# A windowed-attention and FFN kernel: a token tile's work is cut into five parts that are issued between the score steps

## The reference

```
x  = layernorm(x)
disp = x @ W_disp   (16 heads x 16);   val = x @ W_val   (16 heads x 64)
strain[t, j] = disp[t - 63 + j] - disp[t]                       # j = 0..63
bond   = gelu(strain @ W_strain + rel[j] @ W_pos) @ W_bond
damage = sigmoid(gelu(strain @ W_dmg + b_dmg) @ W_dmg_out + b_dmg_out)
w = softmax_j(bond - 10 * damage);   att = (sum_j w * val[t - 63 + j]) @ W_cproj
x = x + att
y = layernorm(x); yp = y shifted by one token
out = x + sigmoid((mu_r*y + (1-mu_r)*yp) @ W_r) * (square(relu((mu_k*y + (1-mu_k)*yp) @ W_k)) @ W_v)
```

## Time and profile before

| | |
|---|---|
| median of 3 runs | 3383.02 us (3380.91 to 3383.12) |
| the profiled execution | 3383.59 us, of which the slowest core's span is 3381.7 us |
| spans of the eight cores | 3370.0 to 3381.7 us |
| busy on the slowest core | PE 1703.1, DVE 915.1, ACT 909.3 us |
| tiles 1 to 5 | about 163 to 329 us of the span |
| chunks 0 to 2 with tiles 6 to 17 | about 330 to 1425 us |

### The profile page before, as it was taken

One profiled execution on the slowest core, in us unless ns is written; L12 is line 12 of the kernel. 1 busy time (PEld: TensorE's weight loads), 2 busy tenths in 40 slices (PEclk: granted clock), 3 DMA queues, 4 the chain that ended last, 5 costly groups with the idle time before them and its releaser, 6 DMA issues.

```text
span 3381.7 us, 21888 instructions; the slowest of 8 cores (3370.0 to 3381.7 us)
## 1 busy us (share of the span) xinstructions
PE 1703.1 (50%) x4568; PEld 468.0 (14%) x4568; DVE 915.1 (27%) x2635; ACT 909.3 (27%) x1269; POOL 8.3 (0%) x15
## 2 busy tenths in 40 slices
PE   0054454545554545265555555566634736547367
PEld 0011111111111111011111221222210101101011
DVE  0012333343335333433333222211121030120301
ACT  0001555355554555044440223200011011110110
POOL 0000000000000000000000000000000000000000
PEclk9999656555555565556555555555555555555555
DMA  7500000010001000120001111111210110100101
GB/s 117 104 23 24 10 10 10 4 19 10 10 10 22 10 10 10 19 50 25 25 25 44 35 35 32 37 43 49 56 38 6 38 38 13 55 7 25 44 6 44
DMA packets 133861, 100.42 MB, mean 30 GB/s; under 512 B 110304, under 2 KB 111472, under 8 KB 133744
## 3 DMA queue, kind: packets, MB, share of 16 engines
q1 hardware_dynamic: 126784, 87.80, 9.8%
q0 software_dynamic: 6960, 11.24, 2.4%
HBM read 74.86 MB, written 35.40 MB: 33 GB/s over the span
## 4 chain that ended last, share of the span: by engine, by line
PE 41%; ACT 21%; issue 20%; DVE 12%; DMA 5%; DVEq 1%; ACTq 0%; SPq 0%
ACT s_actT L377 10%; ACT s_actT L367 5%; PE ps L610 5%; PE ps L264 5%; PE ps L708 5%; PE ps L754 5%; PE ps L733 5%; DMA Ebuf<-s_zero 4%; PE ps L386 3%; PE ps L282 2%; DVE s_eh L444 2%; PE ps L542 2%; PE ps L546 2%; PE ps L568 2%; PE ps L562 2%
## 5 line engine op out<-in xcount | busy, mean ns | idle before, releaser
L386 PE MATMUL ps<-s_actT,s_bd 128*32 128x512 bf16 (+1 forms) x1280 | 445.0, 494 | 393.8 <-ACT s_actT L377 325.7
L377 ACT ACTIVATE s_actT<-s_argT,s_pcols 128x512 bf16<-128x512 bf16 (+1 forms) x640 | 368.3, 646 | 13.5 <-ACT s_actT L377 0.4
L377 ACT ACT_TABLE_LOAD x20 | 25.7, 1283 | 914.6 <-DVE s_argT L356 914.6
L367 ACT ACTIVATE s_actT<-s_argT,s_bdmgc 128x2048 bf16<-128x2048 bf16 x128 | 256.3, 2002 | 16.2 <-PE ps L386 7.3
L356 DVE TENSOR_TENSOR s_argT<-s_dS 128x512 bf16<-128x512 bf16 (+1 forms) x640 | 203.5, 379 | 150.5 <-ACT s_actT L377 124.3
L356 DVE TENSOR_TENSOR s_argT<-s_dD 128x512 bf16<-128x512 bf16 (+1 forms) x640 | 203.5, 379 | 146.7 <-ACT s_actT L377 101.1
L708 PE MATMUL ps<-s_xk,s_wkT 128*128 128x512 bf16 x256 | 149.6, 584 | 158.7 <-DVE s_xk L698 76.9
L386 PEld LDWEIGHTS ps<-s_actT,s_bd 128*32 128x32 bf16 x1280 | 123.2, 117 | 712.6 <-issue 693.5
L250 PE MATMUL ps<-s_ident,s_lntok 128*128 128x128 bf16 x136 | 35.9, 264 | 341.2 <-DVE s_lntok L193 323.5
L264 PE MATMUL ps<-s_wval,s_lnfm 128*128 128x512 bf16 x272 | 158.8, 584 | 58.9 <-DVE s_lnfm L254 20.8
L610 PE MATMUL ps<-s_wcp,s_atok 128*128 128x512 bf16 x272 | 158.9, 584 | 57.2 <-DVE s_atok L588 19.1
(11 more groups left out here) (99 smaller groups left out, 1213.9 us busy)
## 6 DMA issues: line engine op xcount, KB each, us to landing
s_wbt<-Ebuf SPq DMA_DIRECT2D x17, 764.0 KB, 5.4
Ebuf<-s_zero SPq DMA_DIRECT2D x16, 544.0 KB
X2buf<-s_xrel SPq DMA_DIRECT2D x17, 512.0 KB, 2.6
s_x<-X2buf SPq DMA_DIRECT2D x17, 512.0 KB, 3.8
s_xt<-xs SPq DMA_DIRECT2D x33, 256.0 KB, 3.9
s_xrel<-xs SPq DMA_DIRECT2D x33, 256.0 KB, 4.2
s_x2r<-X2buf SPq DMA_DIRECT2D x16, 512.0 KB, 3.7
out<-s_x2r SPq DMA_DIRECT2D x16, 512.0 KB, 2.7
```

Of the source, the lines that this page charges most:

```text
L367: P.emit("scalar", (lambda half=half: (lambda e: e.activation(out=s_actT[:, 2048 * half:2048 * half + 2048], in_=s_argT[:, 2048 * half:204 ...
L377: P.emit("scalar", (lambda slot=slot, W=W, bias=bias: (lambda e: e.activation(out=s_act[slot][:, 0:W], in_=s_arg[slot][:, 0:W], func=AF.Ge ...
L386: (lambda e: e.matmul(PS[bank][32 * q:32 * q + 32, 0:W], s_bd32[:, pi * 128 + v * 32: pi * 128 + v * 32 + 32], s_act[slot][:, 0:W], start= ...
```

## The change

`emit_tile` is cut into five functions: `part_ln` (load and LayerNorm), `part_te` (transposes and their copy), `part_val`, `part_disp` and `part_dsd` (the four small matmuls). Their instructions are the same. One wait differs: the transposes of tile b wait for the `val` copies of tile b-1 and no longer for its last copies.

Before chunk 0 only tiles 1 to 4 are issued, sorted by tile number plus 0, 1, 1.5, 2 or 2.5 for the five parts, so that parts of neighbouring tiles alternate. The parts of tiles 5 to 17 go into a queue, 65 in all. In chunks 0 to 2 one part is taken from it after every four steps and one after each combination, that is five for a group. A group thus gets the LayerNorm behind its first bond steps, the transposes behind its first damage steps, `val` behind its second bond steps, `disp` behind its second damage steps and before the combination, and the small matmuls behind the combination. That is 60 parts, tiles 5 to 16; tile 17 follows whole behind chunk 2's dump.

```
-    def emit_tile(b):
+    sv_dscr = {}
+    def part_ln(b):
...
+    def part_te(b):
+        lnt = s_lntok[b % 2]
         bank = b % 2
-        wtp = {"sv": max(ln_done[b], lnfm_evac.get(b - 2, 0), dSD_evac.get(b - 1, 0)),
+        wtp = {"sv": max(ln_done[b], lnfm_evac.get(b - 2, 0), val_evac.get(b - 1, 0)),
...
+    def part_val(b):
...
+    def part_disp(b):
...
-        sv_dscr = P.now("sv")
+        sv_dscr[b] = P.now("sv")
+    def part_dsd(b):
         for m in range(2):
...
-                waits={"sv": max(sv_dscr, P.now("sv"))}, inc="st")
+                waits={"sv": max(sv_dscr[b], P.now("sv"))}, inc="st")
...
+    TPARTS = (part_ln, part_te, part_val, part_disp, part_dsd)
+    TKEYS = (0.0, 1.0, 1.5, 2.0, 2.5)
...
+    pop_hook = [lambda: None]
...
                             Gc[0] = G
+                        pop_hook[0]()
                 st_pair = P.now("st")
...
                 comb_sv, comb_ss = P.now("sv"), P.now("ss")
+                pop_hook[0]()
...
-    for b in range(1, 6):
-        emit_tile(b)
-    emit_chunk(0, [lambda b=b: emit_tile(b) for b in (6, 7, 8, 9)])
-    emit_chunk(1, [lambda b=b: emit_tile(b) for b in (10, 11, 12, 13)])
-    emit_chunk(2, [lambda b=b: emit_tile(b) for b in (14, 15, 16, 17)])
+    for _, b, i in sorted((b + TKEYS[i], b, i) for b in range(1, 5) for i in range(5)):
+        TPARTS[i](b)
+    PQ = [(b, i) for b in range(5, NTB) for i in range(5)]
+    PQc = [0]
+    def pop_part():
+        if PQc[0] < len(PQ):
+            b, i = PQ[PQc[0]]
+            PQc[0] += 1
+            TPARTS[i](b)
+    pop_hook[0] = pop_part
+    emit_chunk(0)
+    emit_chunk(1)
+    emit_chunk(2)
+    while PQc[0] < len(PQ):
+        pop_part()
+    pop_hook[0] = lambda: None
```

More of the change, by code:

```diff
@@ L305, in emit_tile @@
         dSD_evac[b] = P.now("sv")
+    TPARTS = (part_ln, part_te, part_val, part_disp, part_dsd)
+    TKEYS = (0.0, 1.0, 1.5, 2.0, 2.5)
+    def emit_tile(b):
+        for pf in TPARTS:
+            pf(b)
     ctxB = contextlib.ExitStack()
```

## The result

The change makes the kernel slower: 3479.38 us median against 3381.91 us, a ratio of 1.029 (95% interval 1.0278 to 1.0301). The forecast was 3480 us, within 3440 to 3515. The profiled execution took 3480.25 us, and its slowest core has a span 97.0 us longer than before. These are its rows of the page: the span, the two Gelu lines and the table load at the boundaries (the changed kernel's L393, L383 and L402 are L377, L367 and L386 of before).

The account below looks back on a forecast made before the run. ScalarE was taken to bound the groups inside, the tile's serial chain their boundaries. Groups +94, start -42.8, tile 17 +47.3, less about 2 us, on 3383.6 gave 3480 us, range 3440 to 3515.

Parts of the forecast that it names:

- a part hides nothing: In each group: parts are reached only after the Gelu ends, so ScalarE idles; stalls sum to 45.8 against 37.4 us.
- the `val` gap: Behind a group's second four bond steps: ScalarE stalls 16.3 us, of which val itself is 12.4 us.
- The Tanh's gap: Ahead of the combination: the Tanh waits for disp's last matmul, adding 7.2 us to the earlier 1.43 us.
- The ledger: Whole kernel: groups, start and tile 17 together +98.5 us, less about 2 us for fast PE matmuls.
- the groups: Chunks 0 to 2: four groups at +8.4 us and eight at +7.5 us make +94 us.
- the start: Ahead of chunk 0: first Gelu at 288.7 us instead of 331.53, -42.8 us, mostly from tile 5 moving into chunk 0.
- tile 17: Behind chunk 2's dump with nothing beside it: 8.8 us dump DMAs, 4.7 us load, 33.8 us tile, +47.3 us.
- The clock: PE in the groups: last damage step's matmuls fast at 1.02 us, tile matmuls slow except about 2 us saved.
- The faster clock for `val`: Rival: val matmuls behind steps run at PE's fast level, 66 us less, down to 3414 us; chance 0.08.
- Four table loads in a group: ScalarE: Sqrt and Gelu around the LayerNorm, Exp and Gelu around the combination; 1.28 us each, no extra drain.
- The Square behind a Gelu: LayerNorm on ScalarE: would cost 12 x 1.28 = +15 us if it needed a table load, otherwise nothing.
- The parts hide after all: Rival: three PE parts a group each lie beside up to two steps' Gelus, 166 us less, 3314 us; chance 0.04.

Follow-up runs that it names:

- e4: Changed kernel with each in-group part issued behind the fourth step's Gelu but ahead of its four matmuls: 3421.02 us, ratio 1.0123.
- e5: Changed kernel with the subtractions of step G+2 issued ahead of the part behind step G: 3350.31 us, ratio 0.9911.
- e7: Changed kernel with only the last of every eight tile matmuls (transposes, val, disp) counted on the semaphore: 3256.24 us, ratio 0.9634.
- e1: Changed kernel with all five parts of a tile taken together behind each combination: 3383.76 us, ratio 1.0014.
- e9: Changed kernel with two-step subtraction lead, uncounted tile matmuls, tiles 1 to 5 ahead, val and disp halved, a part behind each second step: 3057.39 us, ratio 0.9045.
- e6: Kernel before the change with only the last of every eight tile matmuls (transposes, val, disp) counted on the semaphore: 3165.47 us, ratio 0.9366.
- e10: Changed kernel with only the LayerNorm behind a group's first four steps and the four other parts behind the combination: 3374.75 us, ratio 0.9976.

## Why the prediction was right

- *That a part hides nothing* held in full. Over the 12 groups the `val` gap is 16.45 us in eleven and 16.73 in one (forecast 16.3), the LayerNorm's 8.7 (8.4), and the transposes' 6.81 to 8.00, mean 7.21 (7.0). The Tanh's gap is 8.04 to 9.43, mean 8.43 (1.43 + 7.2), the small matmuls' 6.9 in chunk 0 and 5.7 in chunk 1 (6.9 and 5.6). The reason given for it was tested from three sides: e4 moves the part in PE's list, e5 the subtractions in VectorE's, and e7 shortens the part, where the cuts in the groups still cost 81 us.
- *The ledger*: the groups +95.2 us (forecast +94, less 2), the start -42.4 (-42.8), tile 17 +47.8 (+47.3). The sum is 100.7 at chunk 3's first Gelu, counted from the first table load; that load came 2.9 us earlier in this execution, and the second half took 0.8 us less. The +95.2 is what the sum leaves beside the other two; e1, which leaves the cuts out, has 93 to 96. That the time of 3480 us came out within 1 us is in part luck: the groups were 3.2 us dearer than forecast, and the earlier load gave 2.9 back.
- *The clock* was only half as I had it. I had taken fast matmuls in the last damage step and slow transposes. The four matmuls took 1.02 us in 8 of the 12 groups; they took 1.86 or 1.87 in three of chunk 0, of which the rows above show one, and 1.69 in one of chunk 1. The transposes were fast in all twelve, eight in 2.78 to 2.92 us where they took 3.16 before. In the group of the rows the granted clock was 0.5 through the four damage steps and 0.97 over the transposes (408.2 to 411.2 us), and back at 0.5 over `val`. The line view has it for the whole run:

```profile
L254 PE MATMUL ps<-s_ident,s_lntok x136: 216/217/267, 165.7 to 1497.3; 128*128 128x128 bf16 x136
...
L269 PE MATMUL ps<-s_wval,s_lnfm x272: 583/583/587, 170.1 to 1509.8; 128*128 128x512 bf16 x136
```

Most transposes took 216 to 217 ns; by the page their mean is 232 ns, and 264 ns before. I had set 2 us for fast transposes and `disp` matmuls, and the busy time of the two is 8 us less (99.6 for 107.8). It nearly makes up for the slow steps: the transposes' stall is 7.2 us for the 7.0 forecast. In chunk 0, with its slow steps, a group without a compaction costs 9.0 us more than before (forecast 8.4), in chunks 1 and 2 7.2 (7.5). The faster clock for `val`, a rival, did not come: 583 ns in the median.
- *Four table loads in a group* are there, each 1.28 us, and the instruction behind starts 0.01 to 0.02 us later. The Square behind a Gelu had no load, so that term is nothing. By the Trainium skill, "ScalarE: Activation LUTs", section "What ACT_TABLE_LOAD costs", a drain of about 1380 ns comes with every switch, and the 12 more would have cost 32 us (an estimate from its 2.66 us for both). The traces do not agree. In the change a drain could still lie in ScalarE's idle time ahead of a load; in e5, where the next step's inputs are already there, the Gelu's load stands 0.08 us behind the Sqrt:

```profile
383.34 0.29 ACT L189 ACTIVATE s_lncol<-s_lncol,s_cst 128x1 f32<-128x1 f32 x1
383.71 1.28 ACT L393 ACT_TABLE_LOAD   x1
```

- *The parts hide after all* fell for the change as it is, and what it said of the mechanism held when VectorE's list was put in the order it needs: 166 us had been the price of two covered steps for each of three parts, and e5, with two parts that have steps behind them and a shorter LayerNorm, gained 129. The Trainium skill's "Perfetto Trace Analysis", section "Optimization Strategy", says that interleaving regimes with different bounds may improve a kernel. The change alone, which interleaves and is slower, does not refute that, and e9, 108 us below e6 with its old order, agrees with it.

## What to carry to other kernels

Cutting a serial chain into pieces between the steps of a pipeline hid nothing by itself here. Look at each in-order list: a piece lies beside the pipeline only if the next steps' inputs are issued ahead of its last wait, and each cut otherwise costs one more emptying and refilling of the pipeline, unless, as in e10, it lets another piece lie beside the combination. Add up the idle time of all lines of the engine that should be busy, since a large wait that shrinks may only have been split.

## What the runs showed of the hardware

The 512-column matmuls that each wait for the one before ran slow: `val` has 583 or 584 ns in nearly every one of its 272 instances, before and after. At 554.6 to 566.3 us of the kernel before PE is busy with them for 80% of the time, and the granted clock is 0.5 throughout, the 1.2 GHz level. The wait alone does not rule out the fast level: the transposes of the changed kernel wait in the same way, and those that came just behind damage steps, with a granted clock of 0.97 in the group shown, mostly took 216 to 217 ns.

Counted only at the eighth, `val` was faster as far as the clock rose. In e6 the eight matmuls of a tile's first half took 3.57 us in 15 of 17 tiles, at a granted clock of 0.5 where the trace has it, and those of the second half 1.89 to 3.00 us. In e9, in the groups, a half stands behind step matmuls, and all 24 took 1.89 us (0.24 us a matmul) at a granted clock of 1.0.

So e6's 214 us have two causes. An estimate from the rows: eight uncounted matmuls at the slow level take 3.57 us for `val` and 1.01 us for the transposes and `disp`, where eight counted ones took 5.72 and 3.16 us. Over 34, 17 and 34 such eights the saved waits are worth 183 us, near the 190 that I had, and 28 us are the faster clock. The whole is a larger effect than the change studied here, and the second half's lines (L610, L708, L733, L754) still have the counted form; that was not tried.
